# Two gated cross-attentions: products per head on 64x64 quarters of the array in place of folded weights

## The chip, the cores and the metric

One core of a Trainium2 chip runs the whole program. The metric is the device time of one execution in microseconds (us), the median of several.

## What is computed

The input x has 128 batches of 64 tokens with 128 features; the context has 64 rows of 96 features for each batch. Two layers follow one another, each a gated cross-attention and a gated expert layer. The part of the reference that the change is about:

```python
q = (x @ Wq).reshape(B, S, HEADS, DIM_HEAD).transpose(0, 2, 1, 3)
k = (context @ Wk).reshape(B, L, HEADS, DIM_HEAD).transpose(0, 2, 1, 3)
v = (context @ Wv).reshape(B, L, HEADS, DIM_HEAD).transpose(0, 2, 1, 3)
attn = jnp.einsum('bhsd,bhld->bhsl', q, k) * scale
attn = jax.nn.softmax(attn, axis=-1)
out = jnp.einsum('bhsl,bhld->bhsd', attn, v)
out = out.transpose(0, 2, 1, 3).reshape(B, S, INNER)
return out @ Wo + bo
...
x = x + jnp.tanh(g_xattn[0]) * _L0_xattn_ref(_layernorm(x, axis=-1), ctx_768, ...)
x = x + jnp.tanh(g_ffn[0]) * _L0_ffn_ref(_layernorm(x, axis=-1), ...)
x = x + jnp.tanh(g_xattn[1]) * _L1_xattn_ref(_layernorm(x, axis=-1), ctx_768, ...)
x = x + jnp.tanh(g_ffn[1]) * _L1_ffn_ref(_layernorm(x, axis=-1), ...)
```

The first attention has 8 heads of 64, the second 16. The first expert layer selects tokens for 16 experts by a Sinkhorn iteration and a top 32; the second picks two of 8 experts per batch.

## The kernel before

The tokens lie in 64 tiles of 128, two batches in each, with tokens on partitions. Stages follow one another: weight folding, the first attention loop, the token selection (`select_tokens`), the experts (`run_experts`), the second attention loop, the last layer. Each stage gives every engine a program of its own; semaphores join them. The order of the work on an engine is the order in which `body` is written, and `pipeline` repeats `body(j)` over steps.

**Folded weights.** Per head, q·k is x Wq Wkᵀ cᵀ. `fold_weights` makes the products Wq Wkᵀ of each head once (`AT`, 96x128 per head) and Wv Wo (`Bw`, 96x128 per head), so the loop never forms q, k or the heads' outputs. Both are kept as two half-precision parts, high and low, and so are the context (`cT`), the values (`vB`) and the probabilities (`Ph`, `PT`); a product of two such operands is three matmuls (high by high and the two mixed ones). Where one operand is single precision (`x`, `u`), a plain single-precision matmul is used.

**A unit** `Unit(j, k)` is one tile with 8 heads (`g` is the group of 8), k steps behind step j. There are U = 64 units in the first loop and U = 128 in the second. On TensorE `body(j)` forms
- `keys` (L629): psU, 8 heads x 3 matmuls x 2 halves of the output columns, from AT and cT, for unit j
- PV (L673): psY, 24 matmuls from PT and vB, for unit j-4
- `values` (L618): psV, two groups of 6 matmuls over 512 columns from cT and Bw, for units j-2 and j-3
- the scores (L697): psS, 4 single-precision matmuls over 256 columns from xT and u, for unit j
- the transposes of the normalised tokens (L645, psX) and, in the first loop, of the context (L685, psC), once a tile.

`half(b)` takes one half of the partitions or columns; two matmuls that write different halves of the output stand next to each other everywhere. ScalarE copies psU to `u` (L742), the high parts of the values (L720), the tokens (L729), takes the exponential (L758) and the high part of the probabilities (L768); in the first loop it also takes the context's high part (L733). VectorE takes maxima and differences (L860, L863), sums and reciprocals (L850, L852), the low parts of the values (L841) and adds psY to x (L856). GpSimd scales (L820), takes the low part of the probabilities (L814) and of the context (L796), and splits the experts' weights (L808, L811). SyncE transposes Ph into PT by DMA (L563).

**Keys ahead.** While the selection runs, TensorE forms the key products of one of the two groups of heads for the first AHEAD = 52 tiles (`form_keys`, L239 through `matmul3`) and stores them in `keys_ahead`. The second loop reads them back for its odd units (`loaded`), so of its first 104 units half form no keys; the last 24 form all. The folds of the second attention are made in the selection too, in `fold`, `fold_products` and `fold_rest`.

## Time and profile before

| what | value |
|---|---|
| three runs | 1917.74 us median, 1917.61 to 1919.73 |
| span of the profiled execution | 1918.0 us |
| TensorE (PE) matmuls, busy | 1812.8 us, 95% |
| TensorE weight loads (PEld) | 1311.9 us, 68% |
| VectorE (DVE) | 1609.1 us, 84% |
| ScalarE (ACT) | 1564.4 us, 82% |
| GpSimd (POOL) | 662.4 us, 35% |
| first loop / selection / experts / second loop | about 18 to 328, 330 to 459, 459 to 1297, 1297 to 1790 us |

The profiler gives for that execution the span alone, and no other time of its own; the span is 0.3 us from the median of the runs. Busy time is the union of an engine's instructions, and a matmul's end is modelled, so in a group of matmuls the time from the start of one group to the start of the next says what the group costs. "Idle before" names what ended a wait.

### The profile page before, as it was taken

To read this page: it belongs to the slowest core of one execution; us is meant where nothing else is said; L and a number is where in the kernel's file an instruction comes from. 1 tells how busy PE (TensorE), PEld (TensorE's weight loads), DVE (VectorE), ACT (ScalarE), POOL (GpSimd) and SP (SyncE) were. 2 spreads that over 40 slices of the span, in tenths; PEclk is the share of its full clock that TensorE was granted. 3 is DMA by queue.
4 is the path that set the end of the run, shared out by engine and by line. 5 is a ranking of instruction groups with operands and counts; after the bars stand their busy time and mean duration, and the time that the engine had idled before them with its cause. 6 is when DMAs were issued, how large, how long until landed. Compare 5 with 4: busy or idle time off the path is not lost. (4 is left out here: it accounts for less than half of the span.)

```text
span 1918.0 us, 72744 instructions
## 1 busy us (share of the span) xinstructions
PE 1812.8 (95%) x28635; PEld 1311.9 (68%) x28635; DVE 1609.1 (84%) x3645; ACT 1564.4 (82%) x2773; POOL 662.4 (35%) x918
## 2 busy tenths in 40 slices
PE   6999998896999999999999999998999999999898
PEld 4777776542666666666666666766777777777677
DVE  5999987598788888888888888778999999988744
ACT  5899997575998989898989989876888888888543
POOL 4788887231000000000000000004666666655565
PEclk8999999897999999999999999999999999999899
DMA  7644545495000000000000001004665555533233
GB/s 180 130 99 93 103 94 102 139 364 187 14 11 15 13 14 11 15 13 15 10 14 14 13 12 52 2 2 107 153 169 154 144 156 147 154 69 72 64 111 121
DMA packets 312954, 160.67 MB, mean 84 GB/s; under 512 B 236558, under 2 KB 295862, under 8 KB 312374
## 3 DMA queue, kind: packets, MB, share of 16 engines
q1 hardware_dynamic: 312278, 157.95, 31.4%
q8 instruction: 130, 2.13, 0.5%
q14 instruction: 66, 0.54, 0.1%
q10 hardware_dynamic: 480, 0.05, 0.0%
HBM read 62.33 MB, written 36.83 MB: 52 GB/s over the span
## 5 line engine op out<-in xcount | busy, mean ns | idle before, releaser
L1793 DVE TENSOR_TENSOR h<-g,h 128x1024 f16<-128x1024 f32 x256 | 313.3, 1224 | 138.3 <-ACT h L1725 138.0
L239 PEld LDWEIGHTS psE<-ew,h 128*128 128x128 f16 x6144 | 351.2, 98 | 56.0 <-issue 40.1
L239 PE MATMUL psE<-ew,h 128*128 128x128 f16 x6144 | 365.2, 219 | 12.8 <-DVE eo L1803 6.0
L1720 ACT ACTIVATE g<-psH,eb1T 128x512 f32<-128x512 f32 x512 | 330.2, 680 | 30.9 <-PE psH L239 24.5
L814 POOL TENSOR_TENSOR Ph<-E,Ph 128x512 f16<-128x512 f32 x192 | 222.0, 1156 | 235.9 <-ACT Ph L768 235.9
L1866 POOL MEMSET rbias<- 64x384 f32 x1 | 0.4, 411 | 839.2 <-POOLq L133 839.2
L1725 ACT ACTIVATE h<-g 128x1024 f16<-128x1024 f32 x256 | 270.6, 1057 | 8.1
L720 ACT ACTIVATE vB<-psV 128x512 f16<-128x512 f32 x384 | 225.9, 589 | 51.2 <-PE psV L618 49.0
L841 DVE TENSOR_TENSOR vB<-psV,vB 128x512 f16<-128x512 f32 x384 | 248.4, 678 | 1.1 <-ACT vB L720 1.0
L618 PE MATMUL psV<-shared 96*64 96x512 f16 x1536 | 209.9, 379 | 1.5 <-DVE vB L841 1.5
L820 POOL TENSOR_TENSOR E<-E,rden 128x512 f32<-128x512 f32 x192 | 199.7, 1040 | 15.1 <-DVE rden L852 14.3
L239 PE MATMUL psH<-shared,ew 128*128 128x512 f16 x768 | 178.1, 382 | 0.0
L239 PE MATMUL psH<-xg,ew 128*128 128x512 f16 x768 | 176.9, 380 | 0.0
L673 PE MATMUL psY<-vB,PT 128*64 128x128 f16 x4608 | 163.9, 220 | 5.4 <-DMA PT<-Ph 5.1
L860 DVE TENSOR_REDUCE top<-psS 128x8 f32<-128x512 f32 x192 | 131.8, 687 | 37.6 <-PE psS L697 37.0
L673 PEld LDWEIGHTS psY<-vB,PT 128*64 128x64 f16 x4608 | 144.8, 111 | 19.6 <-DMA PT<-Ph 10.6
L758 ACT ACTIVATE E<-E,zero_col 128x512 f32<-128x512 f32 x192 | 137.9, 718 | 18.5 <-DVE E L863 15.1
L863 DVE TENSOR_TENSOR E<-psS,top 128x512 f32<-128x512 f32 x192 | 132.8, 691 | 7.8
L697 PE MATMUL psS<-shared,xTa 128*64 128x256 f32 x1024 | 133.5, 381 | 2.4 <-DVE E L863 2.4
L850 DVE TENSOR_REDUCE den<-E 128x8 f32<-128x512 f32 x192 | 130.2, 678 | 5.0 <-ACT E L758 4.0
L239 PEld LDWEIGHTS psH<-shared,ew 128*128 128x128 f16 x768 | 70.2, 98 | 93.5 <-issue 18.7
L239 PEld LDWEIGHTS psH<-xg,ew 128*128 128x128 f16 x768 | 69.9, 98 | 89.9 <-issue 12.7
(308 smaller groups left out, 3417.9 us busy)
## 6 DMA issues: line engine op xcount, KB each, us to landing
keys_ahead<-shared SPq DMA_DIRECT2D x52, 512.0 KB, 4.8
shared<-keys_ahead SPq DMA_DIRECT2D x52, 512.0 KB, 3.6
rawe<-in_L_ffn_w_dram SPq DMA_DIRECT2D x32, 256.0 KB, 3.1
wb<-rw SPq DMA_DIRECT2D x64, 128.0 KB, 2.0
rows<-places SPq DMA_DIRECT2D x110, 64.0 KB, 2.5
out_dram<-x SPq DMA_DIRECT2D x7, 512.0 KB, 3.2
context_T<-shared SPq DMA_DIRECT2D x64, 48.0 KB, 2.4
PT<-Ph SPq DMA_TRANSPOSE x192, 2.8
```

The source lines that it names most:

```text
L239: last = e.matmul(to, a, b, start=start and n == 0, stop=stop and n == 2, **flags)
L618: last = e.matmul(a.values(b)[half(hp)], cT[:, a.ring, cl, half(b)], Bw[:, bl, a.g, hp].rearrange("p k d -> p (k d)"), start=n == 0, stop= ...
L673: last = e.matmul(psY[half(b), 0:D], PT[:, a4.par, pl, pair, half(b)], vB[:, a4.par, vl, b, pair, :], start=a4.g == n == pair == 0, stop=a ...
L697: last = e.matmul(psS[half(b), h:h + 4, :], xT[:, a.tp, half(b)], u[:, a.slot, h:h + 4, half(b)], start=True, stop=True)
L720: e.activation(vB[:, a.par, 0, b].rearrange("p k d -> p (k d)"), a.values(b), ACT.Copy).then_inc(s["vh" + name], 1)
L758: e.activation(E[:, a1.four], E[:, a1.four], ACT.Exp, bias=zero_col[:], scale=DH ** -0.5)\
L814: e.tensor_tensor(Ph[:, a2.par, 1].rearrange("p k t -> p (k t)"), E[:, a2.four].rearrange("p h l -> p (h l)"), Ph[:, a2.par, 0].rearrange( ...
L820: e.tensor_tensor(E[:, a1.four], E[:, a1.four], rden[:, a1.par, :].unsqueeze(2).broadcast_to([P, 8, N]), ALU.mult)\
L841: e.tensor_tensor(vB[:, a.par, 1, b].rearrange("p k d -> p (k d)"), a.values(b), vB[:, a.par, 0, b].rearrange("p k d -> p (k d)"), ALU.sub ...
L1720: e.activation(g32[:, ft, :], psH[:, ft, :], ACT.Gelu_apprx_tanh, bias=b1T[:, a.expert(1) * FT + ft:a.expert(1) * FT + ft + 1]).then_inc(s ...
L1725: e.activation(h[:, 1 - par, 0, ft - 1:ft + 1, :], g32[:, ft - 1:ft + 1, :], ACT.Copy).then_inc(s["h_hi"], 1)
L1793: e.tensor_tensor(h[:, 1 - par, 1, 2 * q:2 * q + 2, :], g32[:, 2 * q:2 * q + 2, :], h[:, 1 - par, 0, 2 * q:2 * q + 2, :], ALU.subtract)\
```

## The change

The folded weights go. Both loops now form q and k (`project`, psQK), the scores from them per head (psS), the values per head (psV), the heads' outputs (psO) and the output product with Wo (psY). A head has 64 features, so psO and psS have 64 rows to sum over and 64 columns out: each of these matmuls names one half of the rows and one half of the columns of the array, a quarter of 64x64. `keys_ahead` now holds k for all 16 heads of the 52 tiles, so all of the first 104 units (`a.ahead`) form q only. psQK, psV and psO have one buffer each. ScalarE copies both halves of the projections (`projected`), psO, and the values in one pass in place of two; VectorE takes the values' low parts in one pass and the tokens' low part; GpSimd makes both parts of the context. Units are one step deeper: psY is five behind. VectorE and GpSimd take sums and scaling a step later than before. In the selection ScalarE and GpSimd split the plain weights where folds stood. The diff, with removed lines left out where the kernel above shows them:

```diff
-    AB1 = shared[0:DC, 0:64 * D].rearrange("p (w l g k) -> p w l g k", w=2, l=2, g=2)
...
-    u1 = shared[:, 64 * D + 8 * P:64 * D + 8 * P + 6 * 8 * P].bitcast(F32).rearrange("p (s h l) -> p s h l", s=3, h=8)
+    WQ1 = shared[:, 0:16 * P].rearrange("p (l g k d) -> p l g k d", l=2, g=2, k=4)
+    WK1 = shared[0:DC, 16 * P:32 * P].rearrange("p (l g k d) -> p l g k d", l=2, g=2, k=4)
+    WV1 = shared[0:DC, 32 * P:48 * P].rearrange("p (l g h k) -> p l g h k", l=2, g=2, h=2)
+    WO1 = shared[:, 48 * P:64 * P].bitcast(F32).rearrange("p (g k h d) -> p g k h d", g=2, k=2, h=2)
...
+    KL1 = shared[:, 72 * P:104 * P].bitcast(F32).rearrange("p (s k l) -> p s k l", s=2, k=8)
+    O1 = shared[:, 104 * P:120 * P].bitcast(F32).rearrange("p (s h k) -> p s h k", s=2, h=2)
...
-    def fold_weights(s, G, raw, wqT, wkT, wvT, AT, Bw, psW, psA, psB):
...
+    def output_rows(Wo, to):
+        frm = Wo.rearrange("(n q h p) d -> q h p n d", q=2, h=2, p=DH)
+        return [(to[DH * q:DH * q + DH, :, :, h].rearrange("p g k d -> p (g k) d"), frm[q, h])
+                for q in range(2) for h in range(2)]
...
+                wq = sb(c, "wq", [P, 2, G, 4, P], F16)
+                wk = sb(c, "wk", [DC, 2, G, 4, P], F16)
+                wv = sb(c, "wv", [DC, 2, G, 2, 4 * DH], F16)
+                wo = sb(c, "wo", [P, G, 2, 2, D], F32)
...
-            xT = sb(c, "xTa", [P, 2, P], F32)
...
+            xT = sb(c, "xTa", [P, 2, 2, P], F16)
+            QK = sb(c, "QK", [P, 2, 2, 4, P], F32)
+            O32 = sb(c, "O32", [P, 2, 2, 256], F32) if first else O1
...
-            psU = ps(c, "psU", [P, 2, 512], F32)
-            psV = ps(c, "psV", [P, 3, 512], F32)
-            psS = ps(c, "psS", [P, 8, N], F32)
+            psQK = ps(c, "psQK", [P, 512], F32)
+            psV = ps(c, "psV", [P, 512], F32)
+            psS = ps(c, "psS", [P, 2, 512], F32)
+            psO = ps(c, "psO", [P, 2, 512], F32)
...
+                        a, a3, a4, a5, nx = (Unit(j, k) for k in (0, 3, 4, 5, -1))
+                        PASSES = ((0, 0), (1, 0), (0, 1))
+                        def project(part):
+                            pairs = range(4) if a.ahead else range(2 * part, 2 * part + 2)
+                            todo = [(wq, xT[:, a.tp], k) for k in pairs]
+                            if not a.ahead:
+                                todo += [(wk, cT[:, a.ring], k) for k in pairs]
+                            for q, (w, moving, k) in enumerate(todo):
+                                for n, (wl, ml) in enumerate(PASSES):
                                     for m in range(2):
...
+                                        last = e.matmul(psQK[half(m), P * q:P * q + P], w[:, wl, a.g, k, half(m)],
+                                                        moving[:, ml, :], start=n == 0, stop=n == 2)
+                            last.then_inc(s[f"U{part}"], 1)
                         if a.on:
...
+                                wait(e, s["xh"], a.t)
+                                wait(e, s["xl"], a.t)
...
+                            if first or not a.ahead and a.j.off > 2 * AHEAD:
+                                wait(e, s["uc1"], a.formed() - 1)
+                            else:
+                                wait(e, s["uc0"], a.j - 1)
+                            project(0)
+                        if a3.on:
+                            wait(e, s["vl"], a3.j - 1)
+                            for b in range(2):
+                                for n, (bl, cl) in enumerate(PASSES):
+                                    for hp in range(2):
+                                        last = e.matmul(psV[half(hp), 256 * b:256 * b + 256], cT[:, a3.ring, cl, half(b)],
+                                                        wv[:, bl, a3.g, hp, :], start=n == 0, stop=n == 2)
+                            last.then_inc(s["V"], 1)
+                        if nx.opens:
+                            wait(e, s["ln"], nx.t)
+                            wait(e, s["xl"], nx.t - 1)
+                            if first:
+                                wait(e, s["ct"], nx.t - 1)
+                            for m in range(2):
+                                last = e.matmul(psX[half(m)], xn[:, nx.tp, half(m)], ident32[:], start=True, stop=True)
+                            last.then_inc(s["X"], 1)
+                        if a.on and not a.ahead:
+                            wait(e, s["uc0"], a.j)
+                            project(1)
+                        if a5.on:
+                            wait(e, s["oc"], a5.j)
+                            if a5.opens:
+                                wait(e, s["res"], a5.t - 1)
+                            for hp in range(2):
+                                for k2 in range(2):
                                     for b in range(2):
...
+                                        last = e.matmul(psY[half(b), 0:D],
+                                                        O32[:, a5.par, hp, P * k2 + 64 * b:P * k2 + 64 * b + 64],
+                                                        wo[:, a5.g, k2, hp, :], start=a5.g == hp == k2 == 0,
+                                                        stop=a5.g == G - 1 and hp == k2 == 1)
+                            last.then_inc(s["Y"], 1)
...
+                            e.wait_ge(s["cc_pad"], 1)
+                            wait(e, s["clo"], nx.t)
+                            wait(e, s["xl"], nx.t)
                             for hl in range(2):
                                 for m in range(2):
                                     last = e.transpose(psC[half(m), hl, :], cc[:, nx.tp, hl, half(m)], ident16[:])
...
+                        if a4.on:
+                            wait(e, s["vl"], a4.j)
+                            wait(e, s["oc"], a4.j - 1)
+                            wait(e, s[f"pt{a4.par}"], ring_of(a4.j, 2, a4.par), 16)
+                            e.sem_inc(s["O_begins"], 1)
+                            for k2 in range(2):
+                                for b in range(2):
+                                    to = slice(P * k2 + 64 * b, P * k2 + 64 * b + 64)
+                                    for n, (vl, pl) in enumerate(PASSES):
+                                        for hp in range(2):
+                                            for kp in range(2):
+                                                k = 2 * k2 + kp
+                                                last = e.matmul(psO[half(kp), hp, to],
+                                                                vB[half(hp), a4.par, vl, b, DH * k:DH * k + DH],
+                                                                PT[half(hp), a4.par, pl, k, half(b)],
+                                                                start=n == 0, stop=n == 2)
+                            last.then_inc(s["O"], 1)
                         if a.on:
...
+                            if a.ahead:
+                                if a.opens:
+                                    wait(e, s[f"ul{a.tp}"], ring_of(a.t, 2, a.tp), 16)
+                                wait(e, s["uc0"], a.j)
+                            else:
+                                wait(e, s["uc1"], a.formed())
                             wait(e, s["sub"], a.j - 1)
...
+                            e.sem_inc(s["S_begins"], 1)
+                            for k in range(4):
+                                keys = KL1[:, a.tp, 4 * a.g + k] if a.ahead else QK[:, a.par, 1, k]
                                 for b in range(2):
...
+                                    for hp in range(2):
+                                        last = e.matmul(psS[half(b), hp, N * k:N * k + N], QK[half(hp), a.par, 0, k, half(b)],
+                                                        keys[half(hp), half(b)], start=True, stop=True)
                             last.then_inc(s["S"], 1)
...
+                def projected(e, a, part, copy):
+                    wait(e, s["S"], a.j - 2)
+                    wait(e, s[f"U{part}"], a.j if part == 0 else a.formed())
+                    if a.ahead:
+                        to, frm = QK[:, a.par, 0].rearrange("p k t -> p (k t)"), psQK[:]
+                    else:
+                        to = QK[:, a.par, :, 2 * part:2 * part + 2].rearrange("p q k t -> p q (k t)")
+                        frm = psQK[:].rearrange("p (q k) -> p q k", q=2)
+                    copy(to, frm).then_inc(s[f"uc{part}"], 1)
...
+                        def copy(to, frm):
+                            return e.activation(to, frm, ACT.Copy)
+                        if a5.on:
+                            wait(e, s["O"], a5.j)
+                            wait(e, s["Y"], a5.j - 2)
+                            copy(O32[:, a5.par], psO[:, :, 0:256]).then_inc(s["oc"], 1)
+                        if a.on:
+                            projected(e, a, 0, copy)
...
+                            wait(e, s["V"], a3.j)
+                            wait(e, s["O"], a3.j - 2)
+                            copy(vB[:, a3.par, 0].rearrange("p b k -> p (b k)"), psV[:]).then_inc(s["vh"], 1)
+                        if nx.opens:
+                            wait(e, s["X"], nx.t)
+                            wait(e, s["S"], nx.j - G - 1)
+                            copy(xT[:, nx.tp, 0, :], psX).then_inc(s["xh"], 1)
...
                             e.activation(E[:, a1.four], E[:, a1.four], ACT.Exp, bias=zero_col[:], scale=DH ** -0.5)\
...
+                        if a.on and not a.ahead:
+                            projected(e, a, 1, copy)
...
+                            copy(Ph[:, a2.par, 0].rearrange("p k t -> p (k t)"),
+                                 E[:, a2.four].rearrange("p h l -> p (h l)")).then_inc(s["phi"], 1)
...
+                            wait(e, s["V"], nx.j - RING)
...
+                            copy(cT[:, nx.ring], psC[0:DC]).then_inc(s["ct"], 1)
+                        if not first and j.reg is None and j.off == 6:
+                            e.wait_ge(s["nmr"], 1)
...
+                        a, a2, fut = (Unit(j, k) for k in (0, 2, -2))
+                        if a2.on:
+                            wait(e, s["rden"], a2.j)
+                            e.tensor_tensor(E[:, a2.four], E[:, a2.four],
+                                            rden[:, a2.par, :].unsqueeze(2).broadcast_to([P, 8, N]), ALU.mult)\
+                             .then_inc(s["mul"], 1)
...
+                        if first and fut.on:
+                            wait(e, s["C"], fut.t - 2)
+                            e.tensor_copy(cc[:, fut.tp, 0, 0:DC], tile_of(fut.t, ctx32)).then_inc(s["chi"], 1)
+                            wait(e, s["chi"], fut.t)
...
+                        if first and fut.on:
+                            e.tensor_tensor(cc[:, fut.tp, 1, 0:DC], tile_of(fut.t, ctx32), cc[:, fut.tp, 0, 0:DC],
+                                            ALU.subtract).then_inc(s["clo"], 1)
...
+                        parts = (0, 8, 16, 32, 48, U)
+                        for lo, hi in zip(parts, parts[1:]):
...
+                    for n, ((frm, hi), (_, lo)) in enumerate(zip(split_parts(0), split_parts(1))):
+                        e.wait_ge(s["w_hi"], n + 1)
+                        e.tensor_tensor(lo, frm, hi, ALU.subtract).then_inc(s["w_lo"], 1)
...
+                    e.dma_start(KL1[:, 0].rearrange("p k l -> p (k l)"), keys_ahead[0]).then_inc(s["next"], 16)
+                    load_all(e, s["next"], [(shared[:, 0:16 * P], parts_q),
+                                            (shared[0:DC, 16 * P:32 * P], parts_kv[0]),
+                                            (shared[0:DC, 32 * P:48 * P], parts_kv[1]),
+                                            (cT1[:, 0].rearrange("p h t -> p (h t)"), context_T[0])]
+                             + output_rows(I["L1_xattn_Wo"], WO1))
+                    e.wait_ge(s["next"], 16 * 9)
```

What TensorE executes per step. In the first loop's last steps before its repeated part, of before (psXC holds psX and psC; the number behind x counts matmuls):

```order
L645 MATMUL psXC<-ident_1,xna 64x128 x2
L629 MATMUL psU<-shared,AT 64x128 x48
L673 MATMUL psY<-vB,PT 64x128 x24
L618 MATMUL psV<-Bw,shared 64x512 x6
L685 MATMUL psXC<-ident_1,cc 64x128 x4
L697 MATMUL psS<-u,xTa 64x256 x4
```

and of the change:

```order
L554 MATMUL psQK<-xTa,wq 64x128 x12
L554 MATMUL psQK<-shared,wk 64x128 x12
L576 MATMUL psV<-wv,shared 64x256 x12
L585 MATMUL psXC<-ident_1,xna 64x128 x2
L554 MATMUL psQK<-xTa,wq 64x128 x12
L554 MATMUL psQK<-shared,wk 64x128 x12
L597 MATMUL psY<-wo,O_1 64x128 x8
L608 MATMUL psXC<-ident_1,cc 64x128 x4
L622 MATMUL psO<-PT,vB 64x64 x48
L640 MATMUL psS<-QK 64x64 x16
```

The projections stand at the head in two groups with the values and psX between them, and psO with its 48 small matmuls is new ahead of the scores. In the second loop, where keys are read back, two steps of before (`shared` holds cT, AT, Bw, u and xn there):

```order
L697 MATMUL psS<-shared,xTa 64x256 x4
L618 MATMUL psV<-shared 64x512 x6
L629 MATMUL psU<-shared 64x128 x48
L673 MATMUL psY<-vB,PT 64x128 x24
L618 MATMUL psV<-shared 64x512 x6
L697 MATMUL psS<-shared,xTa 64x256 x4
L645 MATMUL psXC<-ident_1,shared 64x128 x2
```

and one step of the change:

```order
L554 MATMUL psQK<-xTa,shared 64x128 x24
L576 MATMUL psV<-shared 64x256 x12
L597 MATMUL psY<-shared 64x128 x8
L82 REGISTER_ALU
L622 MATMUL psO<-PT,vB 64x64 x48
L82 REGISTER_ALU
L640 MATMUL psS<-shared,QK 64x64 x16
```

The 48 key products of every second step have become 24 products of q in every step.

## Rows read from the trace of the kernel before

**Rows 1.** Windows: busy us (count) of PE, PEld, DVE, ACT, POOL; clock, DMA share, GB/s.
```profile
200.00:280.00 80.00, 79.79 (x1780) 63.67 (x1777) 73.97 (x162) 75.08 (x176) 65.83 (x89) 1.00 0.48 100
1450.00:1550.00 100.00, 100.00 (x1894) 73.39 (x1890) 97.56 (x191) 85.52 (x165) 63.79 (x68) 1.00 0.56 148
1700.00:1760.00 60.00, 60.00 (x1324) 47.69 (x1320) 51.91 (x100) 50.37 (x99) 33.07 (x36) 1.00 0.34 69
```
**Rows 2.** Timeline, PE, one step of the first loop: start, length, group.
```profile
154.13 1.51 PE L629 MATMUL psU<-shared,AT 96*64 96x128 f16 x48
155.47 0.84 PE L673 MATMUL psY<-vB,PT 128*64 128x128 f16 x24
156.15 0.82 PE L618 MATMUL psV<-Bw,shared 96*64 96x512 f16 x6
156.80 0.28 PE L685 MATMUL psXC<-ident,cc 128*64 128x128 f16 x4
156.91 1.03 PE L697 MATMUL psS<-u,xTa 128*64 128x256 f32 x8
157.78 0.82 PE L618 MATMUL psV<-Bw,shared 96*64 96x512 f16 x6
158.43 0.39 PE L645 MATMUL psXC<-ident,xna 128*64 128x128 f32 x4
158.65 1.51 PE L629 MATMUL psU<-shared,AT 96*64 96x128 f16 x48
```
**Rows 3.** Timeline, PE, second loop, a pair of units with half the keys read back.
```profile
1599.88 1.04 PE L697 MATMUL psS<-shared,xTa 128*64 128x256 f32 x8
...
1607.24 1.04 PE L697 MATMUL psS<-shared,xTa 128*64 128x256 f32 x8
```
**Rows 4.** Timeline, PE, late second loop, a pair of units that form all keys.
```profile
1763.40 1.51 PE L629 MATMUL psU<-shared 96*64 96x128 f16 x48
...
1771.97 1.51 PE L629 MATMUL psU<-shared 96*64 96x128 f16 x48
```
**Rows 5.** Lines L1450 and L1452, 442 to 446 us: count, ns min/median/max, first and last start.
```profile
L1450 PE MATMUL psG<-ident,vals x64: 192/198/217, 442.3 to 443.5; 128*32 128x32 f32 x64
L1452 PE MATMUL psI<-ident,idx x64: 190/196/203, 442.4 to 443.6; 128*32 128x32 f32 x64
```
**Rows 6.** The late burst: line L1452, and the window of its tile with the clock.
```profile
L1452 PE MATMUL psI<-ident,idx x32: 241/241/241, 455.5 to 456.3; 128*32 128x32 f32 x32
...
455.30:456.30 1.00, 0.80 (x32) 0.85 (x32) 0.00 (x0) 0.50 0.00 0
```
**Rows 7.** Timeline, PE, one step of the experts.
```profile
1007.76 2.84 PE L239 MATMUL psE<-ew,h 128*128 128x128 f16 x48
1010.54 0.62 PE L1673 MATMUL psA<-eo,put 64*128 64x128 f16 x16
1010.99 0.38 PE L1598 MATMUL psR<-sel,xne 64*128 64x512 f16 x1
...
1011.31 2.76 PE L239 MATMUL psH<-xg,ew 128*128 128x512 f16 x12
```
**Rows 8.** Timeline, PE, a fold product on row halves in the selection.
```profile
410.42 1.12 PE L1425 MATMUL psZ<-raws,wTs 64*96 64x128 f32 x16
411.47 1.47 PE L239 MATMUL psK<-cTs,xg 96*128 96x512 f16 x6
```
**Rows 9.** Groups by form: count | busy us, mean ns | idle before it.
```profile
L841 DVE TENSOR_TENSOR vB<-psV,vB 128x512 f16<-128x512 f32 x384 | 248.4, 678 | 1.1 <-ACT vB L720 1.0
L1750 DVE TENSOR_TENSOR xne<-xnfe,xne 128x128 f16<-128x128 f32 x56 | 15.9, 284 | 0.5 <-ACT xne L1685 0.5
L796 POOL TENSOR_TENSOR cc<-ctx,cc 128x96 f16<-128x96 f16 x52 | 19.0, 366 | 0.0
```
**Rows 10.** Timeline, weight folding and start of the selection.
```profile
17.15 0.27 DVE L457 TENSOR_SCALAR bo_rep<-bo_rep,tanh_g 128x128 f32<-128x128 f32 x1
...
347.03 2.74 PE L239 MATMUL psF<-cTs,xg 96*128 96x512 f16 x6 [1.70 <-DVE xg L1183]
```

More of the change, by code:

```diff
@@ L623, in keys @@
-                        def keys(a, b):
-                            wait(e, s[f"uc{b}"], a.key() - 1)
-                            for h in range(4 * b, 4 * b + 4):
-                                to = slice(P * (h % 4), P * (h % 4) + P)
-                                for n, (al, cl) in enumerate(((0, 0), (0, 1), (1, 0))):
-                                    for m in range(2):
-                                        last = e.matmul(psU[half(m), b, to], AT[:, al, a.g, h, half(m)],
-                                                        cT[:, a.ring, cl, :], start=n == 0, stop=n == 2)
-                            last.then_inc(s[f"U{b}"], 1)
@@ L633, in body @@
-                        nx = Unit(j, -1) if first else a
-                        def ready():
-                            if first and nx.on:
-                                wait(e, s["clo"], nx.t)
-                                wait(e, s["xt"], nx.t)
-                        def tokens():
-                            if nx.opens:
-                                wait(e, s["ln"], nx.t)
-                                wait(e, s["ct" if first else "xt"], nx.t - 1)
-                                for m in range(2):
-                                    last = e.matmul(psX[half(m)], xn[:, nx.tp, half(m)], ident32[:], start=True,
-                                                    stop=True)
-                                last.then_inc(s["X"], 1)
@@ L1026, in select_tokens @@
                 psG = psF[:, 0, 0:NE]
-                folded = [psF[0:DC].rearrange("p h (k d) -> p h k d", d=D)] \
-                    + [AT[:, hl].rearrange("p (k h) d -> p h k d", h=2) for hl in range(2)]
                 with nc.Block() as block:
```

504 lines of the change are left out of this document (128 added, 376 removed).

## The prediction

> **What bounds the kernel now.** I read the stage table first [rows 1]. In both attention loops TensorE is busy for the whole of a stretch (79.8 of 80 us, 100 of 100, 60 of 60) at a granted clock of 1.00, which is 2.4 GHz. VectorE has 2% left in the stretch of the second loop where half of the key products are read back (97.6 of 100 us), and 8 to 13% elsewhere; ScalarE has 6, 14 and 16% left. TensorE's own order of time shows how closely its work is packed [rows 2]: one unit (128 tokens, 8 heads) runs from one key-product group to the next, 154.13 to 158.65, 4.52 us, and the starts of its groups give 1.34 us for the 48 key products psU, 0.68 for the 24 products psY, 0.65 for each of two value groups psV, 0.11 for the context's transposes, 0.87 for the scores psS, 0.22 for the token transposes psX. These add up to 4.52: no wait is left over. In the second loop a pair of units whose keys are half read back takes 1599.88 to 1607.24, 7.36 us, so 3.68 each [rows 3]; late in that loop, with nothing read back, a pair takes 1763.40 to 1771.97, 8.57, so 4.29 each [rows 4]. There are 64 units of the first sort, 104 of the second and 24 of the third. So TensorE's time per unit sets 192 periods, and the change is worth what it does to that.
>
> **What it does to TensorE, group by group.** Prices from rows 2. A small half-precision matmul on one half of the array's columns costs 1.34/48 = 28 ns when the two halves alternate; a record of a 128-column single-precision one 0.22/4 = 55 ns (each single-precision matmul leaves two records).
> - Out, in the first loop: psU 1.34, psY 0.68, two psV 1.30, psS 0.87. Sum 4.19. The 0.33 for psX and psC stay.
> - q and k, new: 24 + 24 matmuls of the shape of psU: 1.34. With keys read back only the 24 of q: 0.67.
> - Values, new: 12 matmuls over 256 columns in place of 12 over 512: half of 1.30, so 0.65.
> - psY, new: 8 single-precision matmuls, 16 records of 128 columns: 16 x 55 ns = 0.88.
> - psO, new: 48 matmuls on quarters of 64x64 that stream 64 columns. Nothing in the trace has this shape. From below: 64 columns are half of what psU streams, and four quarters run where two halves did, so 28/4 = 7 ns each, 0.34 us. From above: they start no faster than psU's, 28 ns, 1.34 us. The nearest row is the burst psG/psI with its four 32-column strips: 128 records, each a load and a matmul, start from 442.3 to 443.6, which is 10.2 ns each [rows 5]. At a granted clock of 0.50 the 64 records of the late burst, 32 of them psI, start within 0.9 us, 14 ns each [rows 6], what streaming alone asks there (64 cycles at 1.2 GHz, over four strips, 13.3); loading was hidden. At full clock streaming would ask 6.7 and it took 10.2, so I take 10.2 as the pace at which such pairs start, and psO as 48 x 10.2 = 0.49.
> - psS, new: 16 single-precision matmuls on quarters, 32 records of 64 columns. Half of 55 ns over twice as many places is 14 ns, above that pace: 0.44. From above 32 x 28 = 0.90.
> - Changes of tiling, new: whole columns before, quarters for psO and psS, back. In the experts the same kind of change occurs [rows 7]: two 512-column matmuls side by side take 1010.99 to 1011.31, 0.32, where rows 2 give 0.65/3 = 0.22, and the 48 ahead of it take 2.78 where 48 x 56 ns are 2.69. That is 0.2 for a round trip; in the token selection 16 records on row halves take 1.05 against 0.88 [rows 8], 0.17. I take 0.2; bounds 0 and 0.4, which also hold the two semaphore increments that TensorE's queue now carries ahead of psO and psS and that no row prices.
> The Trainium skill, "TensorEngine Tiling (Array Packing)", section Key Properties, says that changing the tiling mode drains TensorE; the trace agrees, with those 0.2 us.
>
> First loop: 1.34 + 0.65 + 0.22 + 0.88 + 0.11 + 0.49 + 0.44 + 0.2 = 4.33, against 4.52: -0.19, times 64 = **-12 us**. Second loop, read back: 0.67 + 0.65 + 0.11 + 0.88 + 0.49 + 0.44 + 0.2 = 3.44 against 3.68: -0.24, times 104 = **-25**. Rest: 1.34 + 0.65 + 0.11 + 0.88 + 0.49 + 0.44 + 0.2 = 4.11 against 4.29: -0.18, times 24 = **-4**.
>
> **Do the others keep up?** Per unit of the first loop ScalarE is busy 75.08/80 x 4.52 = 4.24 [rows 1]; it keeps six 512-column passes (psO's copy comes, one of the two value copies goes) and loses the context's copy of 0.27: about 4.0. VectorE, 4.18, loses one 0.68 pass and gains one of about 0.28 on 128x128 [rows 9]: 3.8. GpSimd, 3.72, gains the context's first part, at most the 0.37 of its second [rows 9]: 4.1 at worst, and it also waits each time for ScalarE's half of Ph. All lie under 4.33, GpSimd by little. Where keys are read back, ScalarE needs 0.855 x 3.68 = 3.15 and VectorE 0.976 x 3.68 = 3.59, less 0.68, plus half of 0.28, 3.1: both under 3.44. The cover is thin: without it each 0.1 us is 19 us of the whole.
>
> **New waits.** psQK is one bank. The second half of the projections waits until ScalarE has copied the first; behind that wait on TensorE stand psY, psO and psS. Values (0.65) and psX (0.22) lie between, 0.87 us for a 0.59 copy and its hand-over of some 0.2: just covered, if ScalarE is free when the first half ends. psS waits for the second copy; psY, psC and psO, 1.48 us, lie between. psV and psO are single too; by the order of the groups their copies are due over 1 us ahead of the next use. I cost these at nothing; the first is the one that would show.
>
> **The rest.** Set-up: VectorE leaves it at 17.15 + 0.27 [rows 10], its norm of the first tiles having waited for the folds' first copy. Now that norm starts when x has landed, two fold passes go and three of half their size come: I estimate -4, between 0 and -7. The token selection loses TensorE's 1.7 us wait for the folded keys [rows 10]: -2. The folds behind it and GpSimd's four new passes lie beside VectorE's chain: nothing. Both loops are a unit deeper and end with a copy and psY, 1.5 us each: +3. SyncE's loads before the second loop become nine in place of four, of about the same bytes, issued before the experts' last step: nothing, at worst +5.
>
> Sum: -12 - 25 - 4 - 4 - 2 + 3 = -44, hence 1918 - 44 = **1874 us**. The profiled execution's span of 1918.0 and the median of 1917.7 differ by 0.3, so nothing is added for what lies around it. About 0.2%, 4 us, is what a measurement here tells from no change.
>
> **Rivals.**
> 1. *Quarters do not overlap as strips do* (slower). In rows 5 four strips differ in columns only. In psO two quarters share their columns and differ in rows; if loading one holds up the other, each column half takes its 24 loads in turn, and rows 2 bound such a load by 1.34/24 = 56 ns. psO is then up to 1.34, psS up to 0.90: +1.31 per unit, x 192 = +252, 2126 at the worst; with 40 ns a load psO is 0.96, +90, **1964**. It decides from 44/192 = 0.23 us per unit, when psO passes 0.72 or 15 ns per matmul. Against it: psA and the fold products run on row halves at 28 ns and 66 ns a record [rows 7, 8]. For it: no row has both splits. Chance 0.22, a third of it above 1985.
> 2. *Loading bounds each quarter by itself.* If a 64-column load takes the whole 56 ns of rows 2 but the four overlap, psO takes 12 x 56 = 0.67: +0.18 x 192 = +35, **1909**. The late burst speaks for quicker loads [rows 6]. Chance 0.15. The Trainium skill, "TensorE: Matmul & The Clock Gate", section LDWEIGHTS, prices a load at its columns over 1.2 per ns, an estimate of 53 ns for 64 columns and 0.64 us for psO, and would give 1903.
> 3. *The new waits take TensorE's place*: ScalarE comes 0.15 to 0.2 late to the projections, or GpSimd paces the first loop. +29 to +38, **1903 to 1912**, at the worst no change. Chance 0.1.
> 4. *The quarters cost only their streaming* and the drain vanishes: TensorE asks 3.98 and 3.10, and GpSimd, ScalarE and VectorE set about 4.15 and 3.2 instead: -24 - 50 - 7 with the ends' -3, **1834**. Chance 0.13.
> My forecast, within 15 us of 1874, has 0.40.
>
> **Numbers.** The range takes in rivals 2, 3 and 4 and the milder two thirds of rival 1: 1832 to 1985, with about 0.1 outside. Its faster side holds the likeliest case, by itself 1860 to 1890. Faster by over 0.2%: 0.40 + 0.13 + 0.13 + 0.05 = 0.71; within it 0.05; slower 0.24.
>
> **What would show it.** In the new profile: groups of psQK at 0.67 per 24, psY at 0.88, psO at about 0.49 and psS at 0.44 between starts; periods of 4.33, 3.44 and 4.11; TensorE still busy throughout, with waits under 0.1 us a unit. psO above 0.72 proves rival 1; gaps before the second projection group prove rival 3; VectorE or ScalarE without gaps and TensorE with them prove rival 4. Stages other than the loops should move by under 5 us each; if they don't, the forecast is wrong for another reason.

## The result: 2103.36 us, slower by 9.7%

The changed kernel takes 2103.36 us (median of 4 runs, 2101.62 to 2109.04), the kernel before 1918.6 (4 runs, 1917.61 to 1919.73): a ratio of 1.0967, with an interval of 1.095 to 1.0983. The prediction was 1874 with a range up to 1985. The profiled execution's span is 2100.7. Its page:

```profile
span 2100.7 us, 97246 instructions
...
PE 1856.5 (88%) x40785; PEld 1451.7 (69%) x40785; DVE 1550.1 (74%) x3582; ACT 1553.3 (74%) x2701; POOL 684.5 (33%) x984
...
PE   5899997876999999999999999777778878889898
...
PEclk9999998997999999999999999899999989999899
...
q8 instruction: 273, 4.47, 0.9%
```

Three things stand here. TensorE is busy for 88% where it was 95. The loss of busy time lies in the slices from the 26th on, the second attention loop. And the queue that carries instructions moved 273 packets (16 KB each) where it moved 130 before.

The ends of the stages, from the first or last group of each:

| mark | before | after | step, after less before |
|---|---|---|---|
| first psL of the token selection (end of loop 1) | 333.9 | 355.6 | +21.7 |
| `rbias` cleared (start of loop 2) | 1297.5 | 1322.5 | +3.3 |
| last psY (end of loop 2) | 1798.7 | 1985.5 | +161.8 |
| end | 1918.0 | 2100.7 | -4.1 |

So nearly all is in the second loop. The stage table there, and the view of TensorE's waits from 1350 to 1750 us (engine, tile, line, releaser: us in total, times, longest):

```profile
core 0: us, PE busy (x) PEld busy (x) DVE busy (x) ACT busy (x) POOL busy (x), PEclk, DMA share, GB/s
1350.00:1450.00 100.00, 80.07 (x2662) 71.64 (x2660) 63.59 (x129) 61.54 (x117) 46.93 (x50) 0.93 0.63 116
1450.00:1550.00 100.00, 78.37 (x2634) 69.82 (x2629) 63.86 (x129) 63.21 (x120) 46.28 (x50) 0.95 0.66 120
```

```profile
PE psQK L554 <- issue: 41.6, 9, 5.3
PE psO L622 <- issue: 25.7, 32, 1.7
```

Where TensorE was busy for 100 of 100 us [rows 1] it is now busy for 78 to 80, and VectorE, ScalarE and GpSimd for less than 65. What ends the waits is no engine, no DMA of data and no semaphore: "issue" means that TensorE waited for nothing that the profile shows. Order of time on TensorE through a turn of its loop (8 units; groups between left out):

```profile
1480.73 0.69 PE L640 MATMUL psS<-shared,QK 64*64 64x64 f32 x32
1486.15 1.49 PE L554 MATMUL psQK<-xTa,shared 128*64 128x128 f16 x24 [4.72 <-issue]
1487.42 1.49 PE L576 MATMUL psV<-shared 96*64 96x256 f16 x12
1488.70 1.76 PE L597 MATMUL psY<-shared 128*64 128x128 f32 x16
...
1497.93 0.44 PE L622 MATMUL psO<-PT,vB 64*64 64x64 f16 x31
1499.82 0.34 PE L622 MATMUL psO<-PT,vB 64*64 64x64 f16 x17 [1.45 <-issue]
...
1507.15 0.29 PE L622 MATMUL psO<-PT,vB 64*64 64x64 f16 x12
1508.00 0.48 PE L622 MATMUL psO<-PT,vB 64*64 64x64 f16 x36 [0.57 <-issue]
...
1527.79 1.49 PE L554 MATMUL psQK<-xTa,shared 128*64 128x128 f16 x24 [4.24 <-issue]
```

The rows show two kinds of wait. A long one, 4.1 to 5.3 us, stands once in 8 units, ahead of the body's first group: at the jump back. Short ones stand in the middle of a group of like products, where no semaphore is waited for. And after the long one the same groups take nearly twice their time (psQK 1.27 us to the next group's start, against 0.69): the granted clock is 0.53 there, the 1.2 GHz level, after TensorE was idle:

```profile
1481.50:1486.10 4.60, 0.00 (x0) 0.00 (x0) 1.36 (x2) 0.00 (x0) 1.91 (x3) 0.70 0.72 66
1486.20:1490.40 4.20, 4.20 (x54) 3.88 (x55) 0.69 (x1) 2.04 (x4) 0.00 (x0) 0.53 0.10 24
```

The DMA view of 1450 to 1550 us has the instruction queue at 23 packets, 0.38 MB. The same window of the kernel before has none, nor has the first loop of either kernel in 120 to 280 us.

```profile
q8 instruction: 23, 0.38, 1.7%
```

### The profile page after: what moved, and what is told of

Same layout as the page of the kernel before. It is cut to its first block and busy times, and to the rows that moved or that the text cites. A ratio compares the mean times of both kernels' runs of the same rounds, so it can differ in the third digit from the quotient of the medians.

```text
span 2100.7 us, 97246 instructions
## 1 busy us (share of the span) xinstructions
PE 1856.5 (88%) x40785; PEld 1451.7 (69%) x40785; DVE 1550.1 (74%) x3582; ACT 1553.3 (74%) x2701; POOL 684.5 (33%) x984
## 5 line engine op out<-in xcount | busy, mean ns | idle before, releaser
L1582 ACT ACTIVATE g<-psH,eb1T 128x512 f32<-128x512 f32 x512 | 330.3, 680 | 30.8 <-PE psH L244 24.4
L671 ACT ACTIVATE QK<-psQK 128x512 f32<-128x512 f32 x280 | 166.7, 595 | 221.7 <-PE psQK L554 221.6
L795 DVE TENSOR_TENSOR vB<-psV,vB 128x512 f16<-128x512 f32 x192 | 132.6, 690 | 163.7 <-ACT vB L671 162.0
L554 PE MATMUL psQK<-xTa,shared 128*64 128x128 f16 x3072 | 124.4, 232 | 57.3 <-issue 54.8
L597 PE MATMUL psY<-shared 128*64 128x128 f32 x2048 | 150.1, 287 | 16.7 <-issue 12.5
L622 PE MATMUL psO<-PT,vB 64*64 64x64 f16 x9216 | 120.5, 196 | 33.2 <-issue 31.6
L554 PEld LDWEIGHTS psQK<-xTa,shared 128*64 128x64 f16 x3072 | 99.0, 117 | 71.3 <-issue 56.6
L622 PEld LDWEIGHTS psO<-PT,vB 64*64 64x64 f16 x9216 | 95.1, 109 | 69.2 <-issue 64.8
L597 PEld LDWEIGHTS psY<-shared 128*64 128x64 f32 x2048 | 127.5, 146 | 20.9 <-issue 15.4
```

The lines of the kernel that those rows point to most:

```text
L554: last = e.matmul(psQK[half(m), P * q:P * q + P], w[:, wl, a.g, k, half(m)], moving[:, ml, :], start=n == 0, stop=n == 2)
L597: last = e.matmul(psY[half(b), 0:D], O32[:, a5.par, hp, P * k2 + 64 * b:P * k2 + 64 * b + 64], wo[:, a5.g, k2, hp, :], start=a5.g == hp == ...
L622: last = e.matmul(psO[half(kp), hp, to], vB[half(hp), a4.par, vl, b, DH * k:DH * k + DH], PT[half(hp), a4.par, pl, k, half(b)], start=n == ...
L671: return e.activation(to, frm, ACT.Copy)
L1582: e.activation(g32[:, ft, :], psH[:, ft, :], ACT.Gelu_apprx_tanh, bias=b1T[:, a.expert(1) * FT + ft:a.expert(1) * FT + ft + 1]).then_inc(s ...
```

## The experiments

**Theory A: the code.** In the new kernel TensorE has 273 instructions in an ahead unit (144 before), in the built program 2186 in the repeated body of 8. By this theory they no longer stay in place beside the engine, so each turn fetches them anew. **Theory B:** the stalls come with the quarters, with the two marker increments, or with the single banks.

**1 to 3. The same products, other loops.** The loop of four needed a ring of two context buffers for the ahead units on SyncE and TensorE; the other two change the length of a loop and nothing else:

```diff
-                    pipeline(eng, body, -1, 2 * AHEAD, lo, 2 * AHEAD, RING * G)
+                    pipeline(eng, body, -1, 2 * AHEAD, lo, 2 * AHEAD, n)
...
-                        phases(e, body, U, 8, U - 1)
+                        phases(e, body, U, 8, U - 1, 4)
```

> The kernel after, but TensorE's repeated body of the second loop (units 8 to 103) unrolls 4 units in place of 8: the context's buffers of these units go by turns of two, with one of them waited for ahead of psV. The same products, of the same size, in the same order; TensorE's repeated body falls from some 2160 instructions (8 times 270) to some 1080. Theory A (the loop's code no longer fits beside the engine and is fetched anew each turn, which starves TensorE): the instruction queue's packets fall from 23 or 24 in 100 us of the second loop to 3 or less, the idle time put down to issue nearly vanishes, an ahead unit falls from 5.05 us to 3.6 to 3.8 us, and the whole by 96 x 1.3 = some 125 us, to 1960 to 2000 us. Theory B (the stalls come with quarters themselves, with the marker instructions ahead of psO and psS, or with single PSUM banks handed to and fro): the units stay at 5.0 us and the whole within 1% of 2103 us.

> The kernel before, with TensorE's repeated body of the ahead units of the second loop unrolled 16 units in place of 8, and nothing else: some 2240 instructions in the body in place of 1120. Its products are full size, there are no quarters and no markers. Theory A: it starts to fetch code all through the second loop (20 or more packets of the instruction queue in 100 us, none before) and slows from 3.68 us a unit to 4.3 us or more (80 units in the loop: 50 to 110 us in all, 1970 to 2030 us). If TensorE can fetch 2240 instructions as fast as it runs them at 280 a unit and 3.68 us, there are fetches and hardly a loss. Theory B: within 0.5% of 1918 us.

> The kernel after, with TensorE's repeated body of the first loop unrolled 8 in place of 4, and nothing else: some 2620 instructions in place of 1310. Theory A: the first loop, which fetches nothing now, fetches 20 or more packets in 100 us and slows from 4.8 us a unit to 5.5 us or more (48 units and more in the loop: 35 to 70 us, to 2140 to 2170 us). Theory B: the first loop stays as it is, and the whole within 0.5% of 2103 us.

Measured: loop of four **1972.85 us** (4 runs, 1967.93 to 1975.02; ratio to before 1.0282, interval 1.0264 to 1.0299); the old kernel with sixteen 1968.3; the first loop of eight 2179.3 (one run each). The loop of four in a window where after had 78:

```profile
1450.00:1550.00 100.00, 98.66 (x3643) 89.80 (x3634) 86.14 (x178) 83.90 (x164) 63.82 (x68) 1.00 0.56 148
```

No packet of the instruction queue lies in this window or the next, and the clock is 1.00. The ahead unit (first psS to last, over 103) went from 5.04 to 3.75 us. The kernel before, with no quarter in it, has 15 packets in 1450 to 1550 once its body has 2306 instructions (20 or more were expected), and waits on issue twice in each turn, 2.1 to 3.0 us each time. Beside them stand waits for the transposes of P, of which the kernel before has 0.3 us in the same 300 us (waits of 1350 to 1650 us):

```profile
PE psV L618 <- issue: 11.4, 4, 3.0
PE psXC L645 <- issue: 10.2, 4, 2.8
PE psY L673 <- DMA PT<-Ph: 10.2, 13, 2.1
```

In the first loop of eight (2694 instructions) 20 packets stand in 120 to 200 us, and the loop ends at 413.6 in place of 355.6. Theory A holds in both kernels and both directions; theory B falls, since quarters, markers and single banks all stand in the loop of four. The other 18 us of that third run lie in the second loop, whose code is the same but stands elsewhere: what such a loop costs is not fixed by its text alone.

**4, 5. Is it the jump or the rate?** `n=16`, and a start of the loop at 2 * AHEAD, which leaves none.

> The kernel after with TensorE's repeated body of the ahead units unrolled 16 in place of 8 (some 4320 instructions), and nothing else. The losses so far are 12 turns x 10.9 us (130 us between after and the loop of four), 5 turns x 9.8 us (49 us, the old kernel with sixteen) and 6 turns x 12.7 us (76 us, the first loop of eight). Theory A1 (each turn of a loop that does not fit costs some 10 us, however long it is, because its first instructions have to be fetched after the jump): 5 turns in place of 12, the whole falls by some 7 x 10 = 70 us less what eight more straight units cost, to 2030 to 2060 us, and the large waits on issue stand once in 16 units. Theory A2 (code is fetched more slowly than TensorE runs it, at a cost for each instruction): the unit stays at 5.0 us and the whole within 1% of 2103 us.

> The kernel after with TensorE's ahead units written out straight, with no loop (104 units x 270 instructions), and nothing else. Theory A1 (the jump back costs, straight code is fetched in time): no turns at all, the ahead unit near 3.8 us, the whole near the loop of four, 1975 to 2000 us. Theory A2 (the rate of fetching): all code has to be fetched once as in after, the unit stays at 5.0 us and the whole near 2103 us; the 24 last units, which are straight code in all of these kernels and take 4.9 us where their rows of work sum to some 4.3 us, speak for a part of it.

Measured 2075.8 and 2057.1 us; ahead units of 4.77 and 4.53 us. Both theories hold a part. Without a jump the long waits are gone (the longest on issue is 2.1 us) but the short ones stay, at a granted clock of 0.99:

```profile
1450.00:1550.00 100.00, 82.41 (x2875) 73.51 (x2870) 68.63 (x138) 66.17 (x128) 50.13 (x54) 0.99 0.64 127
```

5745 loads and matmuls in 100 us, 17.4 ns each, is what fresh code reached here, where resident code ran 7277, 13.7 ns each. So being fetched costs 0.8 us a unit (4.53 against 3.75; 84 us in all, 2057.1 against 1972.9), and the jumps 46 us more (2103.4 against 2057.1). The body is passed 12 times, so there are 11 jumps back, where the expectations counted 12 turns: 4.2 us each, with the slow clock behind them. The Trainium skill, "Runtime: NRT & Kernel Launch", section Instruction fetch mechanics, says that a taken branch out of the fetched window stalls, which the 4.7 us agree with; its statements that crossing from block to block is mostly hidden and that kernels prefer full unrolling are not borne out at 13.7 ns an instruction: written out straight the kernel took 2057.1 us, in a loop that fits 1972.9.

**6, 7. How large may a body be?** The ahead units of after, loop of eight, with `PASSES[:1]` and `PASSES[:2]` in psO. Both leave products out, so they are no faster kernels of the same work; the context's buffers stay as in after.

> The kernel after (TensorE's loop of eight ahead units, 2186 instructions in its body by the count of the built program) with two of psO's three passes left out in the second loop's ahead units: psO then holds the high parts' products alone. 64 instructions a unit fewer, a body of 1674 (1320 in the first loop's, which fetches nothing; 2186 fetches all the time). Left out is 0.3 us of products a unit (32 x 9.4 ns). If 1674 instructions still stay in place, the fetches of the second loop vanish and the unit falls from 5.05 to 3.4 us or a little more, the whole to 2103 - 96 x 1.6 = 1950 us. If the limit lies between 1320 and 1674, the unit falls by 0.3 us and what 64 instructions fewer to fetch save at 17 ns each (1.1 us, which holds the 0.3), so to 4.0 us: 2000 us, with 18 or more packets in 100 us.

> As the run before it, with one of psO's three passes left out: a body of 1930 instructions. The Trainium skill's 128 KB of instruction memory (Advanced Engine Details and Errata) at 64 bytes each would hold 2048, so by it this body fits, the second loop fetches nothing and the unit falls to 3.6 us: 1965 us in all. If the limit is lower, the loop fetches 20 or more packets in 100 us, and the unit falls only by 32 instructions x 17 ns = 0.5 us, to 4.5 us: 2050 us.

Measured 1941.9 and 2059.1 us. With 1674 instructions no packet in 1450 to 1650 and a unit of 3.57 us; with 1930, 23 packets in 1450 to 1550 and a unit of 4.66. One of its turns begins as after's do:

```profile
1504.27 1.49 PE L554 MATMUL psQK<-xTa,shared 128*64 128x128 f16 x24 [4.56 <-issue]
```

The limit lies between 1674 and 1930. The 2048 worked out from the Trainium skill ("Advanced Engine Details and Errata", ISA Cache) is too high a bound for this loop; how a body lies on the 16 KB blocks may matter, and was not tried. The run of 1674 shows one thing more: at 3.48 us a unit (1450 to 1650) TensorE waits for the keys' loads, 11.4 us in 1400 to 1700. So had the ahead unit come to the forecast 3.44 us, these loads, which have no term in the prediction, would have been the next to hold it.

**8. The change of tiling.** The loop of four with the block of psY moved between psO and psS.

> The first experiment's kernel (loop of four) with psY put between psO and psS in both loops, and no product added or taken away: TensorE then goes from quarters to full rows and back once more in each unit. By the prediction's term for such a round trip (0.2 us, bounds 0 and 0.4) the ahead unit grows from 3.72 to 3.92 us and the whole by 128 x 0.2 = 26 us, to some 2000 us. If a change of tiling is free, as a rival has it, the unit stays within 0.03 us and the whole within 5 us of 1973; the places of the waits move little, since the copy of psO gets later by psY only for its own successor.

Measured 2053.0 us, most of it not for the reason named. First the ahead units. The two kernels must be compared over whole turns of four units, since at each turn of the loop psQK comes some 0.2 us late, and a pair holds that turn or not. The loop of four takes 14.77 us from 1501.94 to

```profile
1516.71 0.86 PE L566 MATMUL psQK<-xTa,shared 128*64 128x128 f16 x24
```

and with psY in between four units take 15.09:

```profile
1499.91 0.86 PE L566 MATMUL psQK<-xTa,shared 128*64 128x128 f16 x24
...
1501.26 0.39 PE L599 MATMUL psXC<-ident,shared 128*64 128x128 f32 x4
1501.58 0.58 PE L624 MATMUL psO<-PT,vB 64*64 64x64 f16 x48
1502.09 1.09 PE L636 MATMUL psY<-shared 128*64 128x128 f32 x16
1503.11 0.69 PE L654 MATMUL psS<-shared,QK 64*64 64x64 f32 x32
...
1504.43 0.82 PE L590 MATMUL psV<-shared 96*64 96x256 f16 x12
1505.18 0.58 PE L624 MATMUL psO<-PT,vB 64*64 64x64 f16 x48
...
1515.00 0.86 PE L566 MATMUL psQK<-xTa,shared 128*64 128x128 f16 x24
```

That is 0.08 us a unit; over 1450 to 1700 us the mean unit is 3.78 against 3.69. So one round trip more costs 0.08 to 0.09 us: about half of the term of 0.2, inside its bounds, and not free, as the rival had it. It shows where quarters come behind whole columns: psV is followed after 0.75 us by psO where psY followed after 0.66, and psX after 0.32 where it was 0.22.

The whole is 85 us longer by the profiled spans (2051.2 against 1966.1), and 75 of them lie in the first loop, there in 120 to 280 us in one row:

```profile
PE psXC L610 <- DVE xTa L814: 27.9, 27, 1.4
```

There psC waits until VectorE has read psX, in the same bank; psY had been the cover. It is a wait that the prediction had not looked for.

**9. Do the quarters overlap?** The loop of four, psO and psS with the four quarters as the outer loop.

```diff
-                                        for hp in range(2):
-                                            for kp in range(2):
+                            for hp, kp in ((0, 0), (0, 1), (1, 0), (1, 1)):
```

> The first experiment's kernel with psO's 48 and psS's 16 products in another order, in both loops: all of one 64x64 quarter, then all of the next, in place of quarter by quarter in turn. If the quarters run side by side now (theory A: that is why 48 products of 64 columns take 0.45 us, 9.4 ns each), this takes it away: psO goes to 1.2 us or more, psS from 0.63 to 1.2 us or more, the unit by 1.3 us or more and the whole to 2140 us or more. If they do not overlap (theory B), or the order does not matter to it, psO and psS stay at 0.45 and 0.63 us and the whole at 1973 us.

Measured 2202.5 us. Theory A:

```profile
1503.62 1.31 PE L636 MATMUL psO<-PT,vB 64*64 64x64 f16 x45
...
1504.84 1.43 PE L654 MATMUL psS<-shared,QK 64*64 64x64 f32 x31
1506.20 0.86 PE L566 MATMUL psQK<-xTa,shared 128*64 128x128 f16 x24
```

psO and psS together take 1503.62 to 1506.20, 2.58 us, against 1.18 to 1.40 in turn. The whole loses 230 us, 1.2 for each of 192 units. One quarter's products by themselves start 24.9 ns apart (1.12 us for 45); in turn they start 9.4 apart, 2.6 times as fast, so more than two quarters overlap.

**10 to 12. The named parts of the first loop.** The loop of four with VectorE's `xT` ahead of its `vB`; with `projected(e, a, 1, e.tensor_copy)` on VectorE; with the context's high part on ScalarE.

> The loop-of-four kernel with VectorE's low half of xT ahead of its low half of the values in the first loop. TensorE waits there 0.1 us a unit for xT's low half ahead of psC (3.0 us in 160). If that wait is what keeps the first loop's unit at 4.8 us above the 4.6 us of its products, it goes to 4.65 us and the whole from 1973 to some 1965 us; if it is the tail of a chain that psS and psO end next, nothing over 2 us is gained.

> The loop-of-four kernel with one part of the change undone in the first loop: VectorE copies the second half of q and k (512 columns, 0.6 to 0.7 us) behind its xT, and ScalarE only the first half. VectorE is busy for 0.83 of the loop and would be for 0.96. Theory: the part is not what makes the new kernel slow; undone, the first loop gets slower, by 0.2 to 0.6 us a unit (13 to 40 us in all). A rival: ScalarE, at 0.86 busy, is what holds TensorE up in that loop (psQK's copies); then it gets faster by up to 0.2 us a unit, 1960 us.

> The loop-of-four kernel with the other named part undone in the first loop: ScalarE makes the high part of each context tile again, at the head of its step, and GpSimd only the low part. ScalarE is busy for 0.86 of that loop and gets some 0.3 us a unit more, GpSimd 0.4 us less. If GpSimd's part was what made room on ScalarE, the first loop gets slower by 0.1 to 0.4 us a unit, the whole by 6 to 25 us above 1973; if it never mattered, the first loop ends within 2 us of where it ended and the whole within 0.4%.

Measured 1965.9, 1974.5 and 1970.1 us, which single runs cannot tell from the 1967.9 to 1975.0 of the loop of four. Nor can the end of the first loop by itself: it stands at 350.0, 362.3 and 353.3 us, against 352.1 in the loop of four, but at 351.2 to 358.7 in the six kernels whose first loop is the same. From the first psY of that loop to the last, without its uneven beginning, these six take 297.8 to 301.7 us, and the three 295.4, 303.0 and 298.0.

- `xT` first: the wait for xT fell from 3.0 to 0.4 us, and waits for ScalarE's copies came in its place (1.6, 1.4 and 0.5 us in the same 160). By the last measure some 2 us are gained: the tail of a chain, as the expectation's second case has it.
- VectorE with half of the copies: TensorE waits 5.0 us for xT where it waited 3.0, and the loop ends 4 to 11 us later. That is less than the 13 to 40 expected, and not faster, as the rival had it; so that part of the change did no harm, and helped a little if anything.
- Who makes the context's part changes nothing that these runs can tell.

None of the twelve beats the kernel before.

## Why the prediction was wrong

**The step that failed** is "TensorE's time per unit sets 192 periods". The time of the products did; but each unit was priced by its products alone and never by its instructions, though their number was at hand: the ahead unit went from 144 to 273. That pushed one loop's body past what stays in place. It costs 130 us (experiment 1), in 96 of the 192 units. No rival held it; each was a price per product or a wait on another engine. The last 24 units, passed once and so fetched as they run, take 4.84 us in after and 4.88 in the loop of four; one without a wait takes 4.36 (1804.70 to 1809.06), so they too wait on issue, some 12 us in all. The kernel before waits for nothing there (70.0 of 70 us busy in 1715 to 1785, 4.29 us a unit).

**What is left is +48 us between the profiled spans of before and the loop of four.** 18 of them lie in the first loop and 31 in the second, 2 between the loops, and the last stage gives 3 back. Of the 31, 12 are the fetches of the last units. Another 5 are the loop's beginning, where the first psQK waits 4.95 us for VectorE's low part of xT, which the old kernel did not need; the prediction had nothing there, at worst 5, and for another reason. The end costs 5.5 more (20.3 us from the last psS of the loop to the last psY, against 14.8), with 4.5 us of waits for copies of psO. The ahead units were to give 25 back and give nothing, and that is the sizes. A pair of them in the loop of four:

```profile
1499.79 1.04 PE L611 MATMUL psY<-shared 128*64 128x128 f32 x16
1500.76 0.58 PE L636 MATMUL psO<-PT,vB 64*64 64x64 f16 x48
1501.31 0.69 PE L654 MATMUL psS<-shared,QK 64*64 64x64 f32 x32
1501.94 0.86 PE L566 MATMUL psQK<-xTa,shared 128*64 128x128 f16 x24
1502.63 0.82 PE L590 MATMUL psV<-shared 96*64 96x256 f16 x12
1503.29 0.39 PE L599 MATMUL psXC<-ident,shared 128*64 128x128 f32 x4
1503.51 1.04 PE L611 MATMUL psY<-shared 128*64 128x128 f32 x16
1504.48 0.58 PE L636 MATMUL psO<-PT,vB 64*64 64x64 f16 x48
1505.05 0.69 PE L654 MATMUL psS<-shared,QK 64*64 64x64 f32 x32
1505.88 0.86 PE L566 MATMUL psQK<-xTa,shared 128*64 128x128 f16 x24
1506.57 0.83 PE L590 MATMUL psV<-shared 96*64 96x256 f16 x12
1507.23 1.05 PE L611 MATMUL psY<-shared 128*64 128x128 f32 x16
```

| from start to start, us a pair | predicted | measured |
|---|---|---|
| psQK | 1.34 | 1.38 |
| psV | 1.30 | 1.32 |
| psX | 0.22 | 0.22 |
| psY | 1.76 | 1.94 |
| psO | 0.98 | 1.12 |
| psS | 0.88 | 1.26 |
| turn of the loop (psQK at 1505.88) | none | 0.20 |
| change of tiling | 0.40 | inside the other rows, some 0.2 by experiment 8 |
| sum | 6.88 | 7.44 |

With the next pair, which holds no turn, the mean is 3.69 a unit, against 3.68 before [rows 3]: even with its code in place the ahead unit saves nothing. **psS** was mis-sized most. Its 32 records start 19.6 ns apart (0.63 us); the prediction halved a 55 ns record twice, to 14. A pattern fits the three bursts on record: rows 5, psO and psS take 1.3 to 1.5 times the streaming that the prediction works out for them (10.2 for 6.7 ns, 9.4 for 7, 19.6 for 14). It took the excess in rows 5 for a fixed pace instead, below which nothing starts; that came out for psO, which streams as long, and not for psS. Why it is so was not tried. For psO the 10.2 ns from rows 5 were right: its 48 take 0.45 us where nothing follows late (after, 202.85 to 203.30), 9.4 ns each. **Rival 1** (quarters do not overlap) and **rival 2** fall with that and with experiment 9. **The tiling term** was twice too large: a round trip more costs 0.08 to 0.09 us (experiment 8), not 0.2. The Trainium skill ("TensorEngine Tiling (Array Packing)", Key Properties) says that a change of mode drains TensorE; the trace agrees, with that smaller price.

**The first loop** was to save 12 us and 4 in the set-up; it loses 21.7. Half is its beginning. The first psS comes 1.8 us earlier (22.6 against 24.4), but from there to the first psY it is 28.1 us where it was 15.4. The loop is one unit deeper, and in 15 to 60 us TensorE waits 5.5 us for VectorE's xT (once 4.0), 3.7 for ScalarE's copies of psQK and the context, and 1.8 on issue. In the loop of four, whose first loop is the same, that filling takes 24.5 us; from 22 to 32 us its products run at full pace (12 of psQK in 0.36 us), where in after they take nearly twice as long (0.64). So some 3.6 us do not belong to the change. The prediction put the deeper loops at 3 us, at the end only. The rest is 0.18 us a unit, 4.74 against 4.56 (psY to psY over 63). A unit without a wait takes 4.53 (psS at 217.36 to psS at 221.89), not 4.33: psS 0.63, psC 0.23 for 0.11 (the change to quarters stands behind it), psY 0.92. The waits are the rest, 5.3 us in 120 to 280 us: 3.0 for VectorE's xT, 1.0 for a copy of psQK, 1.3 on issue. That is rival 3's size, but VectorE's wait and not ScalarE's. Groups of one unit, and such a wait:

```profile
201.70 1.04 PE L597 MATMUL psY<-wo,O 128*64 128x128 f32 x16
202.61 0.30 PE L608 MATMUL psXC<-ident,cc 128*64 128x128 f16 x4
202.85 0.57 PE L622 MATMUL psO<-PT,vB 64*64 64x64 f16 x48
203.30 0.69 PE L640 MATMUL psS<-QK 64*64 64x64 f32 x32
204.19 0.53 PE L554 MATMUL psQK<-xTa,wq 128*64 128x128 f16 x12 [0.20 <-issue]
...
231.08 0.30 PE L608 MATMUL psXC<-ident,cc 128*64 128x128 f16 x4 [0.34 <-DVE xTa L800]
```

**Rival 4** asked for TensorE to fall below the others; in the loop of four VectorE and ScalarE are at 86 and 84% beside its 99 (1450 to 1550 us). Right were that none of them became the bound, psQK, psV, psX and psO, and the stages that should not move (+3.3 and -4.1 us).

## What to carry over

Before pricing a change that cuts products smaller, count the instructions in each repeated body per engine, and hold them against the largest body that is known to run without fetches: here 1674 was in place and 1930 was not. A wait on issue in the middle of like products, together with packets on the instruction queue where there were none, is that limit; a shorter loop gave 130 us back at the price of another turn for the context's buffers. And a price read from large products does not shrink with them: psS's record was to fall from 55 ns to 14 on quarters and fell to 19.6.

## What was not expected of the hardware

- A repeated body that does not fit costs twice: 4.1 to 5.3 us of waiting at the jump (after, 11 jumps), and some 17 ns an instruction where resident code ran at 13.7. The clock falls with the first: 0.53 of full speed was granted for the 4.2 us after the wait at 1481 to 1486.
- Products on 64x64 quarters do run side by side, given in turn: 9.4 ns for a load and a matmul of 64 columns, against 25 ns (1.12 us for 45) when one quarter's stand in a row.
- A round trip between whole columns and quarters cost 0.08 to 0.09 us (15.09 against 14.77 us for four units).
